# Six local-attention layers: the feed-forward one pair later, residual sums kept in the token buffer, centring behind the sums of squares

## The reference

```
x = attn_layer(shift_tokens(x), Wqkv[i], q_scale[i], k_scale[i], Wo[i]) + x
x = ffn_layer(shift_tokens(x), ln_g[i], ln_b[i], W1[i], b1[i], W2[i], b2[i]) + x

attn_layer: q, k, v of 16 heads x 64; q and k normalised by their length and scaled; rotary
            turn; softmax over the window of 32 tokens and the one before it; out @ Wo
ffn_layer:  xn = (x - mean) / sqrt(var + 1e-5) * g + b
            a, gate = split(xn @ W1 + b1);   a * gelu(gate) @ W2 + b2      (341 inner channels)
shift_tokens: the upper 64 channels are taken from the token before
```

## Time and profile before

| what | us |
|---|---|
| median of 3 runs (7342.56 to 7348.19) | 7343.36 |
| the profiled execution | 7338.15 |
| its span | 7336.3 |
| PE busy in it | 5478.9 |
| DVE busy | 4621.9 |
| ACT busy | 3311.9 |
| POOL busy | 2637.1 |

### The profile page before, as it was taken

One profiled execution on the slowest core, in us unless ns is written; L12 is line 12 of the kernel. 1 busy time (PEld: TensorE's weight loads), 2 busy tenths in 40 slices (PEclk: granted clock), 3 DMA queues, 4 the chain that ended last, 5 costly groups with the idle time before them and its releaser, 6 DMA issues. The chain is left out here.

```text
span 7336.3 us, 228324 instructions
## 1 busy us (share of the span) xinstructions
PE 5478.9 (75%) x94991; PEld 3176.4 (43%) x95226; DVE 4621.9 (63%) x9757; ACT 3311.9 (45%) x6753; POOL 2637.1 (36%) x2351
## 2 busy tenths in 40 slices
PE   5777877454777746888888888888888888888874
PEld 1222222112232214555555555555555555555552
DVE  5666666345555545676676666666666766666764
ACT  1444444121333313555555555555555555555542
POOL 0000000000000005555555555555555555655550
PEclk9999999576898967888888888888888888888885
DMA  3011010002111101001100110011001100110000
GB/s 95 14 20 20 13 20 14 26 0 84 27 20 26 20 8 52 23 23 29 32 23 23 29 32 23 23 29 32 23 23 31 34 23 23 31 29 23 23 19 18
DMA packets 99949, 197.56 MB, mean 27 GB/s; under 512 B 23616, under 2 KB 50048, under 8 KB 99328
## 3 DMA queue, kind: packets, MB, share of 16 engines
q1 hardware_dynamic: 94944, 195.44, 10.3%
q10 hardware_dynamic: 4896, 0.84, 0.1%
HBM read 67.45 MB, written 27.26 MB: 13 GB/s over the span
## 5 line engine op out<-in xcount | busy, mean ns | idle before, releaser
L340 DVE TENSOR_REDUCE a_mpart<-a_pm 128x1 f32<-128x512 f32 (+2 forms) x1904 | 1087.4, 628 | 511.9 <-PE a_pm L412 316.7
L517 ACT ACTIVATE a_probs<-a_ps 128x1024 f32<-128x1024 f32 (+3 forms) x896 | 796.0, 930 | 1123.5 <-PE a_ps L433 856.2
L1219 ACT ACTIVATE w_probs<-w_pa,w_nm,w_rqs 128x64 f32<-128x64 f32 x3072 | 971.2, 415 | 126.3 <-DVE w_nm L1367 124.4
L412 PE MATMUL a_pm<-a_KZ,a_QS 128*128 128x512 bf16 (+3 forms) x1869 | 665.1, 390 | 301.9 <-DVE a_mpart L340 187.7
L1212 ACT ACTIVATE w_sq<-w_pr 128x512 f32<-128x512 f32 x768 | 466.2, 607 | 898.4 <-DVE w_sinb L1355 898.4
L324 POOL COPY a_V<-a_vals 128x288 f32 x32 | 14.5, 452 | 1913.0 <-PE a_po L449 1911.7
L1141 PE MATMUL w_pr<-w_xc,w_w 128*128 128x256 f32 (+1 forms) x1152 | 455.6, 576 | 293.9 <-issue 293.9
L433 PE MATMUL a_ps<-a_QS,a_KS 128*128 128x512 bf16 (+3 forms) x1688 | 514.9, 379 | 140.9 <-DMA a_KS<-k_parts 118.1
L929 POOL TENSOR_TENSOR w_sinb<-w_sinb,w_tabk 128x512 f32<-128x512 f32 x384 | 488.4, 1272 | 283.8 <-DVE w_sinb L1355 283.8
L955 POOL TENSOR_TENSOR w_probs<-w_probs,w_rden 128x512 f32<-128x512 f32 x384 | 392.9, 1044 | 539.0 <-DVE w_rden L1377 539.0
L1355 DVE STREAM_SHUFFLE w_sinb<-w_pr 128x512 f32<-128x512 f32 x768 | 562.6, 733 | 0.0
(11 more groups left out here) (218 smaller groups left out, 10160.9 us busy)
## 6 DMA issues: line engine op xcount, KB each, us to landing
w_Vp<-w_V SPq DMA_DIRECT2D x192, 384.0 KB, 3.7
w_Vp<-w_V SPq DMA_DIRECT2D x192, 128.0 KB, 3.4
a_QS<-q_parts SPq DMA_DIRECT2D x136, 96.0 KB, 3.4
a_KZ<-k_parts SPq DMA_DIRECT2D x136, 96.0 KB, 3.6
a_KS<-k_parts SPq DMA_DIRECT2D x136, 96.0 KB, 3.7
q_parts<-a1p_part SPq DMA_DIRECT2D x48, 128.0 KB, 1.8
k_parts<-a1p_part SPq DMA_DIRECT2D x48, 128.0 KB, 1.8
q_parts<-a2p_part SPq DMA_DIRECT2D x48, 128.0 KB, 1.8
```

What stands on the lines that cost most here:

```text
L340: nc.vector.reduce_max(mpart[:, h, qt, kc:kc + 1], p_m[:, k % 2, 0:width], AX_X).then_inc(max_read, 1)
L412: mm = nc.tensor.matmul(out, QS[:, par, h, qt * P:(qt + 1) * P], KZ[:, par, h, kc * CH:kc * CH + width], start=True, stop=True)
L517: nc.scalar.activation(probs[:, s % 2, 2 * pair:2 * pair + 2, c0:CH], p_s[:, pair, :, c0:CH], ACT.Exp, scale=SM_SCALE).then_inc(exped, 1)
L1219: op = nc.scalar.activation(probs[:, g, t, c, :], s_of(g)[:, t, c, :], ACT.Exp, bias=nm[:, g, t, c:c + 1], scale=scale_of(g)[:, t, c:c + 1])
```

## The change

The finishing of a pair is split in two. `mixing` (output projection, residual, centring, variance, layer norm) stays in turn n for pair n - 2. `feed` (the feed-forward and the second residual) is done for pair n - 3. So there is one more turn, 98; turn 2 is written out, and the loop runs over turns 3 to 93. `ffn_in` is issued in two parts of three products, with `variance` between them. `centre` comes behind `norms`. The variance goes into `p_c[:, 1]`. On VectorE `keep_centred` comes behind denominators 0 and 2, and the layer norm behind `split_norms`. On ScalarE the squares of the centred tokens come behind the copy of the norms, `var_root` behind exponentials 1.

The residual is added in place in `XS`; `x1`, its carry (L1387) and its clearing go away. The layer norm's last operation writes a tile of its own, `xo`, from which `ffn_in` reads. Gain and bias of the norm are loaded a second time, into `vecn`, since at a change of layers they are needed before the rest. `mix` waits for the second residual of the pair before last, which is a turn old; `second_residual` waits for the centring product of the next pair.

```diff
-                    dve.wait_ge(S["x2"], m + PPL + FIRST)
-                    nc.vector.tensor_tensor(x1[64:128, 0:1], x1[64:128, PAIR:PAIR + 1],
-                                            notfirst[64:128, ds(m % PPB, 1)], ALU.mult).then_inc(S["x1p"], 1)
-                    dve.wait_ge(S["x1p"], m + 1 + FIRST)
                     dve.wait_ge(S["y"], m + 1 + FIRST)
                     c = col(m)
-                    nc.vector.tensor_tensor(x1[0:64, 0:PAIR], XS[0:64, ds(c, PAIR)], p_c[0:64, 0, :], ALU.add)
-                    nc.vector.tensor_tensor(x1[64:128, 1:PAIR + 1], XS[64:128, ds(c + 1, PAIR)], p_c[64:128, 0, :],
-                                            ALU.add).then_inc(S["x1"], 1)
+                    nc.vector.tensor_tensor(XS[0:64, ds(c, PAIR)], XS[0:64, ds(c, PAIR)], p_c[0:64, 0, :], ALU.add)
+                    nc.vector.tensor_tensor(XS[64:128, ds(c + 1, PAIR)], XS[64:128, ds(c + 1, PAIR)],
+                                            p_c[64:128, 0, :], ALU.add).then_inc(S["x1"], 1)
...
 TensorE
                     if late:
                         unit(7, n)
-                    if finish:
-                        centre(n - 2)
-                    if late:
                         norms(n)
-                    if finish:
-                        variance(n - 2)
+                    if mixing:
+                        centre(n - 2)
                     if late:
                         turn_norms(n)
-                    if finish:
-                        ffn_in(n - 2, late, attend)
+                    if feed:
+                        ffn_in(n - 3, 0, late, attend)
+                    if mixing:
+                        variance(n - 2)
+                    if feed:
+                        ffn_in(n - 3, 1, late, attend)
...
 VectorE
-                    if finish:
-                        keep_centred(n - 2)
                     if attend:
                         denominator(0, n - 1)
                         denominator(2, n - 1)
+                    if mixing:
+                        keep_centred(n - 2)
                     if late:
                         norm_floor(n)
-                    if finish:
-                        layer_norm(n - 2)
                     if attend:
                         turn_probs(0, n - 1)
                         turn_probs(2, n - 1)
                     if late:
                         norm_newton(n)
                         split_norms(n)
+                    if mixing:
+                        var_term(n - 2)
+                        layer_norm(n - 2)
...
 ScalarE
-                    if finish:
-                        square_x(n - 2)
                     if late:
                         keep_norms(n)
-                    if finish:
-                        var_root(n - 2)
-                    if attend:
-                        exps(1, 1, n - 1)
+                    if mixing:
+                        square_x(n - 2)
                     if late:
                         norm_root(n)
+                    if attend:
+                        exps(1, 1, n - 1)
+                    if mixing:
+                        var_root(n - 2)
```

More of the change, by code:

```diff
@@ L745, in windowed @@
         vecs = sb("vecs", [P, 10])
+        vecn = sb("vecn", [P, 2])
         scales = sb("scales", [P, DEPTH * 4])
@@ L956, in scale_probs, with turn @@
                                             ALU.mult).then_inc(S[f"pn{g}"], 1)
-                def turn(n, attend, finish, late, early, more=True):
+                def turn(n, attend, late, early, more=True):
                     if late:
@@ L1125, in variance, with ffn_in @@
                     pe.wait_ge(S["xsq"], m + 1 + FIRST)
[L1126 to L1131, removed]
+                    nc.tensor.matmul(p_c[:, 1, :], ones[:, :], xsq[:, :], start=True, stop=True).then_inc(S["var"], 1)
+                def ffn_in(m, part, late, attend):
+                    if part == 0:
+                        pe.wait_ge(S["w1"], m // PPL * 16 + 16)
+                        pe.wait_ge(S["xn"], m + 1 + FIRST)
+                    for what, k, bank, at in FFN[3 * part:3 * part + 3]:
                         if at == 0:
                             if late:
-                                pe.wait_ge(S[("sq7", "n2c", "nrm")[bank]], m + 3 + FIRST)
+                                pe.wait_ge(S[("sq7", "n2c", "nrm")[bank]], m + 4 + FIRST)
                             elif attend:
@@ L1154, in ffn_out, with turn @@
                     mm.then_inc(S["out"], 1)
-                def turn(n, attend, finish, late, early):
+                def turn(n, attend, mixing, feed, late, early):
                     if attend:
@@ L1180, in turn @@
                     if late:
-                        spread_norms(n, finish)
+                        spread_norms(n, feed)
                         project_v(n)
-                    if finish:
-                        ffn_out(n - 2, late)
+                    if feed:
+                        ffn_out(n - 3, late, mixing)
                     if early:
```

161 lines of the change are left out of this document (90 added, 71 removed).

## The result

The changed kernel took 7442.3 us (median of 4 runs, 7441.1 to 7444.41) against 7344.3 us for the kernel before (4 runs): ratio 1.0133, 95% interval 1.0118 to 1.0148. It is slower by 98 us, where 63 us less had been forecast. The profiled execution took 7441.1 us in its span, 104.8 more than before's 7336.3; TensorE's mean granted clock fell from 0.858 to 0.838.

A forecast was written before the change was run, and what follows sets the result against it. Two chains ran side by side, TensorE's, partly at 1.2 GHz, ending last and GpSimd's just behind. 7338.15 - 103.5 (steady turns) + 28 (clock) + 9 + 4 (other turns) = 7275.7 us, median 7281, range 7240 to 7362.

The forecast's parts named there:

- best case: Steady turn, rival without a late fall of the clock: a turn of 44.4 us, time 7253 us; chance 0.25.
- `pn2` to the last transpose: VectorE behind `pn2`: transposes 0.05 + 0.62, Newton step and split 1.58, layer norm 2.04, denominators to last transpose 3.79 us.
- second half of values and signal, 2.4 GHz: TensorE behind the last transpose: half of the value products 2.63 us, and 0.07 for the signal.
- values to second residual, 2.4 GHz: Stretch from last value product to second residual: counted as unchanged, 6.80 us in fast turns.
- I take one turn in three at 0.92: Second half of values: 1.2 GHz in a third of turns, 0.92 us more each, +28 us in all.
- the clock stays at 1.2 GHz from the wait before values into V's projection: Slower rival in `values`, `spread_norms` and `project_v`: 1.85 us a turn, time 7419 us; chance 0.13.
- the added wait: In `second_residual`: waiting for a product 20 us earlier hides and costs nothing.
- The layer norm behind `pn2`: VectorE, between split and denominators: 2.04 us at turn 96's length; 0.19 us a turn more at the loop's length.
- C: Experiments' clock theory: TensorE idles twice behind the feed-forward, its clock falls, values and what follows run at 1.2 GHz.
- R1: Experiments' rival theory: the layer norm behind `pn2` is itself the cost, whatever the clock.
- The extra slow turn: Outside the steady loop: turn 3 becomes the first pass, one more slow turn, +9 us (bounds 5 to 12).
- that rival: ScalarE: exponentials 3, held by `var_root`, become the bound; gain 0.15 us a turn, time 7343 us; chance 0.07.

The follow-up runs named there:

- w_both: Changed kernel plus 7 unused 128x512 products before `turn_back` and 14 of 128x256 between the halves of values; 7308.04 us, ratio 0.9949 to the kernel before.
- w_tiny: Changed kernel with the same 21 unused products as `w_both`, each only 8 columns wide; median 7535.22 us, ratio 1.0273, profiled span 7434.2 us.
- w_first: Changed kernel with only the 7 unused 128x512 products before `turn_back`; 7439.79 us, ratio 1.0133.
- w_second_t: Changed kernel with 14 unused 128x256 products between the halves of values and 7 of only 8 columns before `turn_back`; 7390.15 us, ratio 1.0075.
- w_order: `w_both` with the last-coming wait put last in the second residual and in the layer norm's last operation; 7298.82 us, ratio 0.9938.
- lag_only: Changed kernel with the old order on TensorE, ScalarE and VectorE, feed-forward still one pair later, `xo` doubled; 7346.29 us, ratio 1.0005.
- b_inplace: Kernel before with one part of the change alone, the residual added in place in the token buffer; 7333.98 us, ratio 0.9987.
- b_warm2: Kernel before plus unused 128x512 products, 8 before `centre` and 10 before `ffn_in`; 7229.92 us, ratio 0.9845.
- ln_late: Changed kernel with all of the layer norm but its first operation moved behind `scale_k`; 7275.06 us, ratio 0.9904.
- ll_both: `ln_late` plus 7 unused 128x512 products before `turn_back` and 14 of 96 columns between the halves of values; 7133.28 us, ratio 0.9723.
- w_second: Changed kernel with only 14 unused 128x256 products between the halves of values; 8170.0 us, ratio 1.1128.
- w_second10: Changed kernel with only 10 unused 128x256 products between the halves of values; 8257.57 us, ratio 1.1244.
- ln_late_w: `ln_late` plus 7 unused 128x512 products before `turn_back` and 6 of 128x256 between the halves of values; 8148.59 us, ratio 1.1093.

## Why the prediction was wrong

The mechanism of the path was right. `pn2` lies 26.8 us behind the second residual as before, GpSimd does not wait in its rotations, `ffn_in` does not wait, and what is late behind `pn2` is VectorE's transposes, Newton step, layer norm and denominators. `w_both`, whose clock is high from the feed-forward on in nearly all turns, is the turn that I forecast in its best case: 44.37 without a fall. It measured 45.11. The steps, us a turn:

| step | predicted | measured |
|---|---|---|
| second residual to `pn2` | unchanged | 26.81, for 26.77 |
| `pn2` to the last transpose | 8.08 | 8.33 |
| second half of values and signal, 2.4 GHz | 2.70 | 2.87 (`w_both`: 5071.39 to 5074.26) |
| values to second residual, 2.4 GHz | 6.80 | 7.12 (`w_both`) |
| cost of the clock | 0.31 | 46.69 - 45.11 = 1.58 |
| turn | 44.68 | 46.69 |

**The step that failed is the clock's: "I take one turn in three at 0.92".** In the three turns of the windows above the clock was at 1.2 GHz in the values each time, and over all turns the median product with V took 289 ns, for 218 before. Per turn it costs 0.87 behind `pn2` (mean of three turns 12.06, `w_both` 11.19) and 0.67 behind the values (7.79 for 7.12), where the bounds were 0.92 and 0.93. My slower rival, "the clock stays at 1.2 GHz from the wait before values into V's projection", is what happened: 7419 there, 7442 measured. I gave it 0.13 because the clock had come back in the earlier trace rows in spite of idle time. But there `ffn_in` stood behind the gap, with nothing to wait for (5031.18 to 5035.40), and the clock was at 2.4 GHz again from 5034.0, before the values began at 5035.55. The change put both gaps behind `ffn_in`, next to the values. `w_both` and `w_tiny` show that the clock is the cause (value products of 228 and 279 ns), `w_first` and `w_second_t` that either gap is enough (249 and 251 ns). "As gaps of half the time touch the old size" was an estimate of mine, and no run shows a size of gap that decides. In the kernel before the clock fell 1.7 us into the 2.37 before `centre` (at 5020.35) and 2.5 us into the 3.12 before `ffn_in` (5030.59). In the changed kernel it fell 3.0 us into the 3.42 before the norms (5027.32) and 2.1 us into the 2.46 before `turn_back`; a turn earlier it fell 2.0 us behind the end of a gap of 1.61 there, and in `w_first` 1.7 us behind the end of the 2.56.

**Mis-sized terms.** The turn at full clock is 0.74 longer than forecast, 67 us in all. 0.25 lies between `pn2` and the last transpose, 8.33 for 8.08: `xo`'s operation waits for three signals and starts 0.24 later behind the one before it than in the kernel before. With the order changed (`w_order`) 0.17 of it went, and 8.16 were left. 0.17 is in the second half of values. The 0.92 for its slow clock was 0.10 short for a like reason: I took 256 products at 72 a us, 3.55 us, less 2.63, where 256 at 101 a us are 2.53. (At the edges of those windows 21 and 26 products are in flight at 2.4 GHz, 19 and 22 at 1.2 GHz, where I took 22 to 27.) 0.32 stands before the second residual, whose idle time went from 3.96 to 4.27; there I had costed the added wait at nothing because its product is 20 us old. It is there in either order of the two waits, and in `lag_only` too (4.27), while `b_inplace`, in place but without the added wait, keeps 3.96. The wait alone, on the kernel before, was not tried.

**The layer norm behind `pn2`.** I counted it, at 2.04, and took the forecast's gain as what TensorE's slow chain leaves over. The runs show what that comparison hid. The old chain was late because of its clock: `b_warm2` puts it at a mean of 44.36 us a turn against 45.52. There the norm is beside GpSimd's scaling and not behind it. The values end 10.12 us behind `pn2` in one kind of turn (5060.71 to 5070.83) and 10.98 in the other (5104.42 to 5115.40), for 11.19 in `w_both`. So the old order loses 1.16 a turn to the clock and the new one 1.49 by the means (46.69 - 45.20). With the gaps filled the new one is 0.84 longer (45.20 - 44.36), 76 us in 90 turns, and that is the part of the loss that C does not explain. 0.32 of it is the idle time before the second residual; the rest fits R1, the norm's place. `ln_late` against the changed kernel (166 us), and `ll_both` against `w_both` (168 us; 43.24 for 45.20 a turn on average), show the price of that place directly. On the length I had the right end: L1421 took 0.42 us there, beside an idle GpSimd, for 0.60 in the earlier trace rows.

**Outside the steady turn.** The extra slow turn was given 9 us and turn 98 4 us; the second residual of turn 3 is 2.1 us later and what follows that of turn 93 is 2.7 us shorter. Counted between the first row maxima, turns 2 and 3 took 51.15 and 50.70 us, before 53.8 and 45.8. So one more turn is slow, but both are less so than the one before. Exponentials 3 end at 5037.68, 2.57 behind `pn2`, and `var_root` holds nothing up; that rival fell.

**Error as a sum.** 114 us is the clock (1.58 - 0.31, 90 turns), 67 the mis-sized terms, -14 what lies outside the loop: 167, as in 7442.92 - 7275.7 = 167 for the profiled execution's own time.

## What to carry to other kernels

When work is moved so that TensorE is done early, look at where its idle time then lies, not only at how much of it there is: the gap of 2.46 us before `turn_back` was off the path, yet the clock fell to 0.50 at its end (5037.6), and the values behind it were on the path (134 us with both gaps filled). Before counting an engine's wait as what a new order would win, fill its gaps with unused products in the old order: here that alone gave 1.25 to 1.55%, with the feed-forward, the lag and the residual untouched. And an operation that nobody needs soon belongs behind the last signal of the path: moved there and with one gap filled, the changed kernel went from 1.0133 to 0.9714.

## What the runs showed of the hardware

- Two gaps of 2.46 and 1.28 us, with 4.4 us of products between them (5037.95 to 5042.31), went with 13.5 us at a granted clock of 0.50 (5037.60 to 5051.10). Over the whole kernel the median value product took 289 ns, for 218 before; my estimate of 0.92 for half of them at 1.2 GHz stands beside a measured 3.89 - 2.87 = 1.02 (5043.44 to 5047.33, and `w_both`).
- Three of the kernels with added products moved 866 packets on q8 ("instruction"), for 54 or 55 in the others built on the changed kernel, and took 10, 11 and 14% more time (`w_second` and `w_second10` against the changed kernel, `ln_late_w` against `ll_both`). In the loop (3000 to 7000 us) `w_second` moved 658 of them, the changed kernel none. It is not a matter of length alone: with 21 and with 7 added products q8 stayed at 54 or 55, with 14 or 10 between the halves alone, or 7 and 6 in both places, it did not. What decides it stays open.
- Two operations of VectorE on 128x256 took 1.23 and 1.26 us beside GpSimd's scaling (`b_inplace`); beside an idle GpSimd the same two took 0.42 each (5037.77 and 5038.10 in the changed kernel).
- One more satisfied wait in front of VectorE's second residual went with 0.3 us more idle time before it, in either order: 4.27 us in `w_both` and 4.34 in `w_order`, for 3.96 in the kernel before and in `b_inplace`. In front of `xo`'s operation it was 0.28 us in `w_both`, and none in `w_order`.
